# Channels on the partitions in the scan's result of a Mamba-and-experts layer

## The reference, cut

```python
y = ssd(xs, dt, A, Bm, Cm)                 # 8 heads of 64 channels, chunks of 128 tokens
y = y + D_param[None, None, :, None] * xs
y = y.reshape(B, L, D_INNER)               # 512 channels
y = rmsnorm(y * jax.nn.silu(z), mixer_norm_w)
h1 = res + y @ out_proj_w
# in ssd, for each chunk, heads h:
#   Y_diag = (C B^T * L[h]) @ xdt[h]       L[h]: decay between two tokens
#   Y_off  = C @ state[h] * exp(A_cum[h])  state carried over from the chunk before
```

## Time and profile before

| | us |
|---|---|
| median of 3 runs | 730.49 |
| the three runs | 727.5, 730.49, 818.51 |
| the profiled execution, its time | 730.28 |
| the profiled execution, its span | 728.5 |

### The profile page before, as it was taken

How to read it: one execution, slowest core, us unless ns; L and a number is a source line. 1 busy time by engine, 2 the same in 40 slices (tenths; PEclk the granted TensorE clock), 3 DMA queues, 4 the chain that set the end, 5 groups by cost and what they waited for, 6 DMA issues and landing times.

```text
span 728.5 us, 10067 instructions
## 1 busy us (share of the span) xinstructions
PE 691.2 (95%) x2797; PEld 441.1 (61%) x2798; DVE 581.6 (80%) x1473; ACT 237.7 (33%) x479; POOL 222.7 (31%) x379
## 2 busy tenths in 40 slices
PE   5979989999999989999969999999999999999995
PEld 4456665558656765765855666666665555555563
DVE  4889998877866574485776888998998888988882
ACT  1566747585467435324011111111111111111110
POOL 3131322413221241210020333333333343434333
PEclk9979989999999999999989999999999999999998
DMA  9233001100120064032118961111152434434112
GB/s 314 64 116 104 14 1 43 74 1 0 63 113 0 1 205 156 1 126 84 54 30 311 315 193 27 30 29 29 29 163 47 136 74 120 98 89 129 30 23 29
DMA packets 39350, 63.20 MB, mean 87 GB/s; under 512 B 5456, under 2 KB 29072, under 8 KB 39312
## 3 DMA queue, kind: packets, MB, share of 16 engines
q1 hardware_dynamic: 31824, 52.61, 21.0%
q0 software_dynamic: 7488, 10.11, 8.6%
HBM read 52.88 MB, written 9.83 MB: 86 GB/s over the span
## 4 chain that ended last, share of the span: by engine, by line
PE 77%; DVE 11%; issue 3%; POOL 3%; DMA 3%; ACT 3%; POOLq 0%; DVEq 0%
PE ps L1089 23%; PE ps L1110 12%; PE ps L508 5%; PE ps L759 4%; PE ps L785 4%; PE ps L771 4%; PE ps L453 4%; PE ps L1098 3%; PE ps L575 3%; PE ps L632 3%; DMA out_rows<-big 2%; PE ps L522 2%; DVE big L2246 2%; PE ps L1119 1%; DVE big L1662 1%
## 5 line engine op out<-in xcount | busy, mean ns | idle before, releaser
L2246 DVE STREAM_TRANSPOSE big<-big 32x224 f32<-32x224 f32 x560 | 225.5, 403 | 8.4
L1089 PE MATMUL ps<-big 128*128 x512 | 200.1, 544 | 1.3 <-ACT big L1544 0.7
L1089 PEld LDWEIGHTS ps<-big 128*128 128x128 f32 x512 | 97.0, 191 | 89.5 <-issue 87.8
L1110 PE MATMUL ps<-big 128*128 x448 | 102.2, 380 | 1.0 <-DVE big L2246 0.6
L1550 ACT ACTIVATE big<-ps 128x896 f32<-128x896 f32 x36 | 33.0, 917 | 202.5 <-PE ps L1089 179.2
L1110 PEld LDWEIGHTS ps<-big 128*128 128x128 f32 x448 | 82.7, 190 | 11.7 <-issue 1.8
L2297 POOL TENSOR_TENSOR big<-big 128x1 f32<-128x1 f32 x110 | 21.7, 197 | 168.1 <-DVE big L2236 153.6
L453 PEld LDWEIGHTS ps<-big 128*128 128x128 f32 x319 | 39.8, 145 | 38.4 <-issue 27.6
L453 PE MATMUL ps<-big 128*128 128x128 f32 x319 | 52.5, 279 | 7.8 <-ACT big L1192 2.3
L1642 DVE SCALAR_TENSOR_TENSOR big<-ps,big 128x511 f32<-128x511 f32 (+2 forms) x72 | 53.0, 747 | 5.4 <-ACT big L1211 3.4
L2263 DVE TENSOR_TENSOR big<-big,ps 128x896 f32<-128x896 f32 x36 | 39.2, 1088 | 22.4 <-PE ps L1089 20.4
(11 more groups left out here) (231 smaller groups left out, 1002.2 us busy)
## 6 DMA issues: line engine op xcount, KB each, us to landing
big<-in_w SPq DMA_DIRECT2D x36, 896.0 KB, 7.5
big<-cum_rows SPq DMA_DIRECT2D x16, 512.0 KB, 5.4
out_rows<-big SPq DMA_DIRECT2D x4, 512.0 KB, 3.0
xn_rows<-big SPq DMA_DIRECT2D x4, 512.0 KB, 3.1
big<-in_hidden SPq DMA_DIRECT2D x1, 1536.0 KB, 12.4
big<-in_in_proj SPq DMA_DIRECT2D x1, 1288.0 KB, 7.4
big<-in_gate SPq DMA_DIRECT2D x1, 640.0 KB, 13.4
big<-in_up SPq DMA_DIRECT2D x1, 640.0 KB, 8.7
```

What stands on the lines that cost most here:

```text
L1089: last = mm(bank(bk + n)[:, 0:HALF], xT[:, k, :], expert_cols(e, off + k * M + n * HALF, HALF), start=(k == 0), stop=(k == KD - 1))
L1110: last = mm(bank(7)[:, 0:D], hTs[:, half, j * P:(j + 1) * P], expert_cols(e, 2 * KD * M + j * D, D), start=(j == 0), stop=(j == MB - 1))
L2246: last = V.transpose(hTs[c * SQ:(c + 1) * SQ, half, :].rearrange("p (j t) -> p j t", j=MB)[:, :, q * SQ:(q + 1) * SQ], ha[q * SQ:(q + 1) * ...
```

## The change

The result of the scan now has channels on the partitions and tokens in the columns. `diag` and `off_` swap their operands: in `diag` the 64 columns of a head of `xdt` are the weights, even heads on the array's columns 0 to 63 and odd heads on 64 to 127, and the 128 columns of `em` are moved; `off_` becomes four products of 128 columns each (8 instructions). The gate `z_` swaps its operands too (same sizes), so the gate of a sequence is complete only with all four of its products, and `y_` waits for all four. `yT_` and `yT_copy` are gone: y4 is already what `out_` needs as weights. `x_D` has 4 instructions of 128 columns and reads `xc` instead of `xs`. exp(A_cum) now differs along the columns, so SyncE reads the cumulative decays once more (`spread_heads`, two transfers a sequence, 64 partitions x 12 rows of 512 bytes each), and ScalarE takes their exponential in one instruction of 128 x 1536 (`head_decay`). The sum of squares runs across partitions: ScalarE squares, GpSimd folds 512 columns to 256 and 128 (`fold`, two additions), TensorE multiplies by a column of 1/512 (`sumsq`, one moved column), ScalarE adds epsilon (`mean_y`), GpSimd takes the power (`scale_y`). `h` moves to another place in memory. VectorE's order list is unchanged. The diff, cut to its core:

```diff
             def off_(n, c):
-                mm(bank(STATES), xc[n % 2][:, 5, l], st, start=True, stop=True).then_inc(off_ps, 1)
+                for j in range(4):
+                    q = slice(j * P, (j + 1) * P)
+                    last = mm(bank(STATES)[:, q], st[:, q], xc[n % 2][:, 5, l], start=True, stop=True)
+                last.then_inc(off_ps, 1)
...
             def diag(n, c):
                 for hh in range(HEADS):
-                    last = mm(bank(DIAG)[:, hh * HD:(hh + 1) * HD], em[n % 2][:, c, hh * P:(hh + 1) * P],
-                              xdt[:, c % 2, hh * HD:(hh + 1) * HD], start=True, stop=True)
+                    rows = slice(hh % 2 * HD, (hh % 2 + 1) * HD)
+                    last = mm(bank(DIAG)[rows, hh // 2 * P:(hh // 2 + 1) * P], xdt[:, c % 2, hh * HD:(hh + 1) * HD],
+                              em[n % 2][:, c, hh * P:(hh + 1) * P], start=True, stop=True)
...
-            def yT_(n, c):
+            def sumsq(n, c):
+                pe.wait_ge(folded, nth(n, CH, c))
...
+                mm(bank(TURN1)[:, 0:1], junk_y[:, c % 2, 0:P], cst[:, C_MEAN:C_MEAN + 1], start=True, stop=True).then_inc(ssy_ps, 1)
...
+            def spread_heads(n):
+                if n > 0:
+                    sp.wait_ge(off_scaled, n * (CH - 1))
...
+            def head_decay(n):
+                act.wait_ge(decb_in, 32 * (n + 1))
+                A(decb, decb, ACT.Exp).then_inc(decb_ready, 1)
...
+            def fold(n, c):
+                q = junk_y[:, c % 2, :]
+                g.wait_ge(square_ready, nth(n, CH, c))
+                G.tensor_tensor(q[:, 0:2 * P], q[:, 0:2 * P], q[:, 2 * P:4 * P], ALU.add).then_inc(fold_step, 1)
+                g.wait_ge(fold_step, nth(n, CH, c))
+                G.tensor_tensor(q[:, 0:P], q[:, 0:P], q[:, P:2 * P], ALU.add).then_inc(folded, 1)
...
 # TensorE's order
             diag(0, 1)
-            yT_(0, 0)
             front(0, 2)
             xbc_(1, 4)
+            sumsq(0, 0)
             out_(0, 0)
...
             off_(0, 3)
+            sumsq(0, 1)
             out_(0, 1)
-            yT_(0, 2)
             diag(0, 3)
+            sumsq(0, 2)
             out_(0, 2)
             hT_(2)
...
 # ScalarE's order
             decay(0, 3)
+            head_decay(0)
             front(0, 1)
...
             dec_e(1)
-            yT_copy(0, 0)
+            square_y(0, 0)
             x_D(0, 1)
-            square_y(0, 0)
             front(0, 2)
             tap(1, 4)
+            mean_y(0, 0)
             tap(1, 5)
...
 # GpSimd's order
             decayed_x(0, 2)
             plus_x_D(0, 1)
+            fold(0, 0)
+            plus_x_D(0, 2)
             scale_y(0, 0)
-            plus_x_D(0, 2)
             scaled_x(0, 3)
+            fold(0, 1)
             scale_y(0, 1)
             plus_x_D(0, 3)
+            fold(0, 2)
             scale_y(0, 2)
```

More of the change, by code:

```diff
@@ L862, in _ @@
             xbc_(2, 4)
+            sumsq(0, 3)
             out_(0, 3)
@@ L913, in _ @@
             mlp_down(0, 3)
+            sumsq(1, 3)
             out_(1, 3)
@@ L935, in _ @@
             mlp_up(1, 0)
+            sumsq(2, 0)
             out_(2, 0)
@@ L945, in _ @@
             xnT_(0, 1)
+            sumsq(2, 1)
             out_(2, 1)
@@ L1001, in _ @@
             off_(3, 3)
+            sumsq(3, 1)
             out_(3, 1)
@@ L1363, in _ @@
             bt_copy(1)
-            yT_copy(0, 2)
+            mean_y(0, 1)
             square_y(0, 2)
             decay(1, 0)
+            mean_y(0, 2)
             hT0(2)
@@ L1415, in _ @@
             bt_copy(2)
+            mean_y(1, 1)
             decay(2, 1)
-            yT_copy(1, 2)
+            square_y(1, 2)
             gate(0, 3)
@@ L1430, in _ @@
             front(2, 0)
-            yT_copy(1, 3)
             square_y(1, 3)
             dt_e(3)
+            head_decay(2)
             x_D(2, 0)
@@ L1437, in _ @@
             front(2, 1)
+            mean_y(1, 3)
             tap(3, 1)
@@ L1480, in _ @@
             x_D(3, 0)
-            yT_copy(2, 2)
+            square_y(2, 2)
             logits_copy(0)
             gate(1, 5)
-            square_y(2, 2)
+            mean_y(2, 2)
             square_h(2, 0)
@@ L1489, in _ @@
             square_h(2, 2)
-            yT_copy(2, 3)
             square_y(2, 3)
+            mean_y(2, 3)
             square_h(2, 3)
@@ L1494, in _ @@
             decay(3, 3)
+            head_decay(3)
             h2T0(2)
-            yT_copy(3, 0)
             square_y(3, 0)
             xnT_copy(1, 0)
-            yT_copy(3, 1)
+            mean_y(3, 0)
+            square_y(3, 1)
             gate(2, 0)
@@ L1514, in _ @@
             gate(2, 5)
+            mean_y(3, 1)
             x_D(3, 3)
             logits_copy(1)
-            yT_copy(3, 2)
             square_y(3, 2)
-            yT_copy(3, 3)
+            square_h(3, 1)
             square_y(3, 3)
-            square_h(3, 1)
+            mean_y(3, 2)
+            mean_y(3, 3)
             square_h(3, 2)
@@ L2381, in _ @@
             decayed_x(1, 0)
+            scaled_x(1, 1)
+            fold(0, 3)
+            decayed_x(1, 1)
             scale_y(0, 3)
-            scaled_x(1, 1)
             scale_h(0)
-            decayed_x(1, 1)
             scaled_x(1, 2)
@@ L2417, in _ @@
             scaled_x(3, 0)
+            fold(2, 2)
             plus_x_D(2, 3)
+            scale_y(2, 2)
             decayed_x(3, 0)
-            scale_y(2, 2)
+            scaled_x(3, 1)
+            fold(2, 3)
             scale_y(2, 3)
             ln2_scale(1)
-            scaled_x(3, 1)
             scale_h(2)
             decayed_x(3, 1)
+            fold(3, 0)
             plus_x_D(3, 1)
@@ L2437, in _ @@
             scale_y(3, 1)
+            fold(3, 2)
+            fold(3, 3)
             scale_y(3, 2)
```

192 lines of the change are left out of this document (93 added, 99 removed).

## The result

The changed kernel takes 752.93 us (median of 4, 752.11 to 755.65) where the kernel before takes 730.66: the ratio is 1.033 with a 95% interval of 1.0307 to 1.0353. (The ratio leaves out one slow execution of the kernel before, 818.51 us.) It is slower by 3.3%, and 9 us above the upper end of the forecast range. The profiled execution took 753.23 us with a span of 751.2.

A forecast was written before the change was run, and what follows sets the result against it. VectorE was taken to bound the scans of sequence 0 and the start of 1, TensorE from about 143 us. 730.3 + 7.4 - 7.5 + 1 (contention) = 731.2, said as 732 for a likelier slow clock spell; range 714 to 744.

The forecast's parts named there:

- sequence 0: First tight stretch, where the new sum-of-squares chain is late: +7.4 us on VectorE's chain, no TensorE gain against it.
- After that: From diag(1, 0) on: TensorE gains 10.6 us, less waits for later folds and head_decay; together -7.5 us.
- From about 143 us on TensorE's time counts one for one: Second kind of stretch, up to 350 us: any TensorE time saved shortens the run by as much.
- the term that I named and did not count: off_ on TensorE: extra weight loads, at most 8 x 0.03 us more, 12 times, +3 us, left out.
- The first wait: Chunk 0 of sequence 0: TensorE idle 3.7 us for fold(0, 0), making VectorE 3.1 us late.
- the second: Sequence 0: scale_y(0, 0) stands behind plus_x_D(0, 2) on GpSimd, so VectorE's h1_(0, 0) is 6.4 us late.
- The wait for fold(0, 2): Sequence 0: fold(0, 2) behind plus_x_D(0, 3) holds out_(0, 2) and hT_(2), about 1 us.
- a clock of 0.5 right after 73 us: Sign of being wrong: granted clock of 0.5, that is 1.2 GHz, just after the first idle in sequence 0.
- The full rival (+15): Idle spells put TensorE at 1.2 GHz for all of 73 to 103 us: +15, 747 us; chance 0.15.
- diag: Its 16 instructions on TensorE go from 1.73 to 1.10 us, pairs running together; a gain of 0.63 each time.
- fold: GpSimd's additions of 256 and 128 columns: 1.3 us with the wait between.
- head_decay: ScalarE's exponential of the cumulative decays: 1.5 us, four times.

The follow-up runs named there:

- e5: e3 with sumsq behind out_ of the same chunk in five places of TensorE's list: 724.53 us, ratio 0.9958.
- e3: Changed kernel with fold(1, 0), fold(0, 0), scale_y(0, 0) and fold(0, 2) moved ahead in GpSimd's list: 728.78 us, ratio 1.0004.
- e7: Kernel before with heads 4 to 7 of diag left out in sequences 1 to 3: 723.3 us, ratio 0.9936.
- e4: Changed kernel with diag's heads reordered so that neighbours use the same half of the array, but for one step: 752.08 us, ratio 1.0343.
- e6: e3 with diag's heads in the order 0, 2, 4, 6, 1, 3, 5, 7, so not in pairs: 733.82 us, ratio 1.0065.
- e2: Changed kernel with 21 idle products on TensorE filling its wait for fold(1, 0): 750.88 us, ratio 1.032.

## Why the prediction was wrong, and where it was right

By the ratios the changed kernel is 24.1 us slower than the kernel before (22.3 by the medians taken side by side): 12.0 for fold(1, 0), 11.7 for the list of sequence 0, and 0.3 for everything else together. By the medians across the groups the first two are 14.0 and 10.1; each is known to some 4 us. The sum of the prediction had 0.9 in place of that: nothing for fold(1, 0), 7.4 for sequence 0, and -6.5 for the rest.

**The step that failed most is one that is not in the sum: fold(1, 0).** "After that" begins at diag(1, 0) and asks of each later fold whether ScalarE's square is in time. For (1, 0) it is, so I put nothing. But fold stands in GpSimd's list, and the rule that I used for chunk 0 of sequence 0 (what stands before it on GpSimd, and what do those wait for) was not applied here. The trace of before had it all. GpSimd and TensorE before, from 131 us:

```profile
131.39 1.89 PE L632 MATMUL ps<-big 128*128 128x256 f32 x8
132.75 1.21 POOL L2323 TENSOR_TENSOR big<-big 128x512 f32<-128x512 f32 x1 [9.01 <-ACT big L1228]
133.92 2.14 POOL L2312 TENSOR_TENSOR big<-big 128x4 f32<-128x4 f32 x1
...
138.71 1.31 POOL L2335 TENSOR_TENSOR big<-big 128x512 f32<-128x512 f32 x1
```

out_(1, 0), the first line, started at 131.39. plus_x_D(1, 1), the last, ends at 140.0, and a fold of 1.3 us behind it at 141.3: 9.9 us after out_ wants its sum. The chip showed 9.80; the agreement to 0.1 is partly luck, but the size was there to be read.

**"From about 143 us on TensorE's time counts one for one" failed as well.** The saving was real. I added up, from the start of the second diag after 140 us (diag(1, 2)) to that of diag(3, 3), the time from each group of TensorE's instructions to the next, less the waits:

```
us                    before    after      e5
diag                   15.6      9.2      9.2
transposes             13.5     10.1     10.3
sumsq                    -       1.8      1.6
all other products    125.9    129.5    129.4
waits                   2.8      8.0      4.9
from first to last    157.7    158.7    155.4
```

diag and the transposes fall by 9.7 us and sumsq adds 1.8, so 7.9 less: as forecast. Of this 5.2 go to new waits, of which sumsq's own are 5.0 (e5 removes most of these), and 3.6 to the other products, spread over off_, z_, out_, gate and up. For off_ the cause is in the rows: 96 instructions instead of 24 are busy 13.7 us instead of 12.4, the term that I named and did not count. A small part is the clock: behind a wait of 2.54 us before h2T_(2) the granted clock is 0.66 in the stretch from 290 us, where before it is 1.00, and in e3, where it is 1.00 from 150 to 300, the other products take 128.8. The rest stays open. In e7 the other products, transposes included, also took 3.2 us more once diag was halved, and there it is mostly the clock, as the stretches from 260 and 265 show (0.50 and 0.85). So a saving came back first as a wait and then, in some executions, as slower products behind it. TensorE was busy without being alone on the critical path; a 5.0 of 5 in a window does not say what stands 1 us behind it.

**Sequence 0: the mechanism was right, the size was short.** Forecast 7.4 us, measured 10.1 to 11.7. The first wait was found at its place and nearly with its length (3.7, measured 3.29), the second cost 3.8 where 3.3 stood. Two terms were too small. The wait for fold(0, 2) had "about 1 us" and was 2.71. And the clock was only a rival, one that needs the whole of 73 to 103 us at 1.2 GHz, though the first wait alone gave some 7 us of it (an estimate from 0.72 and 0.60 in the stretches from 70 and 75), which is 2.9 us on out_ and xbc_ together. It belonged in the likeliest case, at that size; a clock of 0.5 right after 73 us was also one of the signs that I had named for being wrong. The full rival (+15) did not happen: the windows from 80 to 95 us are at 1.00. But the clock falls again at 95, 100 and 105 (0.66, 0.79, 0.53, then 0.81 and 0.85): some 20 us at 1.2 GHz between 70 and 120 us, if every stretch of 5 us gives 10 us times what its clock lacks to 1; before, the same sum gives 7. What these spells cost in sequence 0 no run shows apart from the waits ahead of them.

**Terms that held.** diag: 1.10 forecast, 1.02 to 1.03 measured, the lower bound. By the Trainium skill (TensorEngine Tiling, Key Properties), changing the tiling mode drains the engine; in this trace at most 0.15 us a diag can be that: 8 pairs at the 0.11 of the earlier trace rows are 0.87, which leaves 0.15 for in and out, not the 0.31 of the earlier trace rows. fold: 1.3 forecast, 0.73 + 0.45 measured, and up to 1.97 + 0.85 beside some of VectorE's instructions (last section). head_decay: 1.5 forecast, 1.47. x_D: 1.1 forecast, 1.26. Contention: 1 us forecast; VectorE's busy time grew by 3.3 over the program, so at most that.

**Terms that were counted and not paid.** head_decay(1) and (3) were to cost 1.2 and 1.0. In e5 head_decay(3) runs from 261.62 to 263.1, while the transposes of h2T_(2) that start at 261.61 had waited 2.96 us for VectorE's h2; no wait of TensorE's is behind it. In the kernel after, TensorE shows no wait before h2T_(0) either.

**The chances.** "Slower" had 0.17, most of it for the clock. The case that came (a sum that stands behind unrelated work in a list) was not among the rivals, though its twin in sequence 0 was in the likeliest case.

## What to carry to other kernels

When a change puts a new link on an engine that runs a hand-written list, each of its places has to be walked, not the tightest one alone: when is its input ready, when does the consumer want it, and when does everything ahead of it in the list end. Here that takes one line of the trace of before for each place, and one of sixteen cost 12 to 14 us.

Work that nothing waits for soon (a sum for a norm) belongs behind the product that is wanted now, also on the engine that computes both; in five places that was worth 3 to 4 us here (e5).

A saving on the busiest engine is worth one for one only until the chains through the others catch up: here 10.4 us taken away gave 2.5 to 5.0 (e7). What the same work is worth can also differ with what stalls around it: 7.8 us more on TensorE did not show in the kernel with the late folds (e4), and cost 4 to 5 us without them (e6), though the two measurements are too wide to be sure of that difference.

## What the runs showed of the hardware that was not expected

Two products with weights of 64 columns on the two halves of the array run together at 128 moved columns too: 16 in 1.02 us. Out of pairs the same 16 take 1.51 (e4), and with weights of 128 columns and 64 moved 1.73.

After a wait of 3.3 us that ended at 72.66 the granted clock was 0.72 in the stretch from 70 us and 0.60 in that from 75; around 9.80 us without work it was 0.73 from 145, 0.50 in both stretches from 150 to 160, that is 1.2 GHz, and 0.91 from 160. Filling the long wait with products kept it at 1.00 and gave back about 3 us of 13 at that place (e2). In e7 taking work from TensorE made it wait longer, and the clock fell where before it was full.

fold's two instructions take 0.72 to 0.73 and 0.45 to 0.46 us where VectorE rests, and also where it runs its convolution (L1657, as at 67.11 in e3). Beside VectorE's L1736 and L1688, which read all their operands from where fold reads its own (big, not ps), they take 0.91 and 1.32 in the changed kernel's trace, and L1688 takes 1.75 there, where it takes 1.22 at 128.12:

```profile
89.38 0.64 DVE L1736 TENSOR_TENSOR big<-big 128x256 f32<-128x256 f32 x1
89.70 0.91 POOL L2357 TENSOR_TENSOR big<-big 128x256 f32<-128x256 f32 x1
89.95 1.75 DVE L1688 TENSOR_TENSOR big<-big 128x1024 f32<-128x1024 f32 x1
90.69 1.32 POOL L2359 TENSOR_TENSOR big<-big 128x128 f32<-128x128 f32 x1
```

The slowest fold of the trace, 1.97 and 0.85 us at 230.45, has L1688 beside its first instruction and L1700, the product y4, beside its second.
